# An expert's four table entries read in one load, one job ahead, by TensorE, ACT and DVE

## The chip, the core and the metric

The kernel runs on one core of one Trainium2 chip. The metric is the device time of one execution in microseconds (us). Engines are named as in the profile: PE is TensorE's matmul stream and PEld its weight loads, DVE is VectorE, ACT is ScalarE, POOL is GpSimd, SP is SyncE. A letter q behind a name (PEldq, DVEq) is that engine's sequencer, which reads instructions, works on registers and hands the rest to its engine.

## The reference, cut to what matters

The whole program is a two-layer block network on x (2 x 1024 tokens, 256 wide). The change touches one of its parts, the first mixture of experts: 16 experts, the best 4 of each token are used.

```python
def _L0_ffn_ref(x, keys, w1, b1, w2, b2, rw, rb):
    diff = x[:, :, None, :] - keys
    dist2 = jnp.sum(diff * diff, axis=-1)
    logits = -dist2 + jnp.einsum('bld,ed->ble', x, rw) + rb
    topv, topi = jax.lax.top_k(logits, TOP_K)
    w = jax.nn.softmax(topv, axis=-1)
    hidden = jax.nn.gelu(jnp.einsum('bld,efd->blef', x, w1) + b1, approximate=False)
    exp_out = jnp.einsum('blef,edf->bled', hidden, w2) + b2
    sel = jnp.take_along_axis(exp_out, topi[..., None], axis=2)
    return jnp.sum(w[..., None] * sel, axis=2)
```

F is 1024, so an expert is a 256 to 1024 to 256 network with a gelu between.

## The kernel before, in words

Two blocks matter, one behind the other, with a barrier of all engines between them.

**`route_phase`** (from line 1291) works out the gates and, on DVE and one partition, a small table `jobs` (int32, 1 x 220) from which the next block is steered. For each used expert in turn it has four entries: `n` (how many blocks of 256 tokens want it), `base` (how many jobs stand before it), `sel` (which expert it is) and `boff` (where its list of blocks stands), and it has the lists `blk` themselves and `pairs`, the number of pairs of experts. `JT` says where each kind begins: the four entries of one expert lie in four different arrays. Here too ACT splits the first expert's weights into a high part (L1340, L1343), and DVE makes the low part of w1 (L1463).

**`experts_phase`** runs jobs, one for each expert and block of 256 tokens. With these inputs there are 37 jobs for eight experts, which have 7, 2, 2, 8, 1, 8, 8 and 1 of them. Each of PE, ACT and DVE runs its own copy of the same nest, `jobs` (L1509): a hardware loop over pairs, in it the two experts of a pair written out (q = 0 and 1, with two sets of weights `ew_0` and `ew_1`), and in each a hardware loop over the expert's n jobs. At the head of each expert the engine reads the four entries with `entry` (`value_load`, L1475), at the head of each job one more, the block's number:

```python
n = entry(eng, "n", p * 2 + q, NB)
base = entry(eng, "base", p * 2 + q, E0 * NB)
sel = entry(eng, "sel", p * 2 + q, E0 - 1)
boff = entry(eng, "boff", p * 2 + q, E0 * NB - 1)
with eng.Fori(0, n) as j:
    blk = entry(eng, "blk", boff + j, NB - 1)
```

What an engine does in a job:

- PE (L1578): 48 matmuls up (8 hidden tiles x 2 halves of the width x 3 products of high and low parts), then 48 down in four groups of 12. Group g down waits for DVE's low part g (semaphore `e_lo`).
- ACT (L1608): eight Gelu activations of 128 x 256, two for a pair of hidden tiles (L1615), from PSUM to `hT`.
- DVE (L1628): for each of the four pairs a cast to the high part (L1633) and a subtraction for the low part (L1635), 128 x 512 each, both from SBUF to SBUF; at the end two updates of X (L1641) from PSUM.

POOL works beside them. At its start it adds eight pieces to X (L1567). Then `split` prepares the weights of the expert after next into the set that has come free: it waits for the last job of that set's expert (`e_down`), then runs a small operation on `eb` (L1541), four casts and four subtractions of 128 x 512 for w1 (L1545, L1551), a small one (L1555), four casts and four subtractions for w2 (L1557, L1561). SP loads the weights from HBM (L1480 to L1482), after POOL's eight adds at first. All matmuls of this block go through a helper, so their line is L1470.

Of the kernel before, what the change touches and what calls it, by code (L numbers as in the profile page):

```python
# [14 lines left out]
ALU = mybir.AluOpType  # L15
# [1235 lines left out]

JT = dict(sel=0, n=17, base=33, free=49, pairs=66, boff=67, blk=84)
JOB = 256
# [4 lines left out]
def route_phase(nc, k):  # L1258
# [4 lines left out]
    with ExitStack() as ctx:  # L1263
# [27 lines left out]
        @block.tensor  # L1291
        def _(pe):
            pe.wait_ge(k.r_G, 1)
            for j in range(EB):
                for w in range(NW):
                    last = nc.tensor.matmul(ps[32 * w:32 * w + 32, LG, :], G[:, j, :], k.hT[:, j, w * W:(w + 1) * W],
                                            start=(j == 0), stop=(j == EB - 1))
            last.then_inc(k.r_lgT, 1)
            pe.wait_ge(k.r_k2, 1)
            for j in range(EB):  # L1300
                last = nc.tensor.matmul(ps[:, KK, 0:E0], k.const("ones"), k2[:, j, :], start=(j == 0),
                                        stop=(j == EB - 1))
            last.then_inc(k.r_kk, 1)
            pe.wait_ge(k.r_lgE, 1)
            for t in range(4):
                last = nc.tensor.transpose(ps[:, LGT, t * P:(t + 1) * P], lgT[:, t * P:(t + 1) * P], k.const("ident"))
            last.then_inc(k.r_lg, 1)
            pe.wait_ge(k.r_wd, 1)
            nc.tensor.matmul(ps[:, CNT, 0:NT * E0], k.const("ones"), k.wE[:, :, :].rearrange("p e i -> p (e i)"),
                             start=True, stop=True).then_inc(k.r_cnt, 1)  # L1310
            for g in range(NW):
                for t in range(4):
                    last = nc.tensor.transpose(ps[0:E0, TR[g], t * P:(t + 1) * P], k.wE[:, :, 4 * g + t],
                                               k.const("ident"))
# [49 lines left out]
        def _(dve):  # L1364
# [27 lines left out]
            for i in range(NT):  # L1392
# [28 lines left out]

            sel, n = sn[:, 0, :], sn[:, 1, :]
            then(nc.vector.tensor_scalar(nj[:, 1, 0:E0 // 2], n[:, 0:E0:2], 0.0, None, ALU.is_gt))
            then(nc.vector.tensor_reduce(one[:, 0:1], nj[:, 1, 0:E0 // 2], AX.X, ALU.add))
# [10 lines left out]
            then(nc.vector.tensor_tensor(hot[:, 1, :], hot[:, 1, :], hot[:, 0, :], ALU.mult))  # L1435
            then(nc.vector.tensor_tensor(jf[:, JT["sel"]:JT["sel"] + E0], sel, hot[:, 1, :], ALU.add))
            then(nc.vector.tensor_scalar(hot[:, 2, :], hot[:, 0, :], one[:, 3:4], None, ALU.mult))
            then(nc.vector.scalar_tensor_tensor(jf[:, JT["boff"]:JT["boff"] + E0], jf[:, JT["sel"]:JT["sel"] + E0],
                                                float(NB), hot[:, 2, :], ALU.mult, ALU.add))
            then(nc.vector.tensor_tensor(n[:, 0:1], n[:, 0:1], one[:, 2:3], ALU.subtract))  # L1440
            jn, jb = jf[:, JT["n"]:JT["n"] + E0], jf[:, JT["base"]:JT["base"] + E0]
# [3 lines left out]
            nc.vector.memset(jf[:, JT["sel"] + E0:JT["n"]], 0.0)  # L1445
            nc.vector.memset(jf[:, JT["boff"] + E0:JT["blk"]], 0.0)
            nc.vector.memset(jf[:, JT["free"]:JT["free"] + 2], 0.0)
            nc.vector.tensor_tensor(jf[:, JT["free"] + 2:JT["free"] + E0 + 1], jf[:, JT["base"] + 1:JT["base"] + E0],
                                    jf[:, JT["base"] + 1:JT["base"] + E0], ALU.max)

# [3 lines left out]
            for e in range(E0):  # L1454
# [19 lines left out]
def job_entry(eng, k, name, at, limit):  # L1474
    return eng.value_load(k.jobs[0:1, bass.ds(at + JT[name], 1)], min_val=0, max_val=limit)  # L1475

# [8 lines left out]
def experts_phase(nc, k):  # L1485

    ps = k.ps
    with ExitStack() as ctx:
# [19 lines left out]

        def jobs(eng, each):  # L1509

            pairs = entry(eng, "pairs", 0, E0 // 2)
            with eng.Fori(0, pairs) as p:
                for q in range(2):
                    n = entry(eng, "n", p * 2 + q, NB)
                    base = entry(eng, "base", p * 2 + q, E0 * NB)
                    sel = entry(eng, "sel", p * 2 + q, E0 - 1)
                    boff = entry(eng, "boff", p * 2 + q, E0 * NB - 1)
                    with eng.Fori(0, n) as j:
                        blk = entry(eng, "blk", boff + j, NB - 1)
                        each(base + j, q, blk, p, sel)  # L1520

# [54 lines left out]
        def _(pe):  # L1576
            pe.sem_inc(k.e_down, TILES)

            def job(n, q, blk, p, sel):
                tok = bass.ds(blk * JOB, JOB)  # L1580
                pe.wait_ge(k.e_s1, p * 2 + (q + 1))
                for f in range(FB):
# [19 lines left out]

            jobs(pe, job)

        @block.scalar
        def _(act):
            act.sem_inc(k.e_act, FB)

            def job(n, q, blk, p, sel):
                for f in range(FB):  # L1610
# [6 lines left out]

            jobs(act, job)

        @block.vector  # L1620
        def _(dve):
# [5 lines left out]

            def job(n, q, blk, p, e):  # L1628
                dve.wait_ge(k.e_down, n * TILES + TILES)
                for g in range(PAIRS):  # L1630
# [3 lines left out]
                    dve.wait_ge(k.e_dhi, n * PAIRS + (g + 1))  # L1634
                    nc.vector.tensor_tensor(lo[:, f, :], hid[:, f, :], hi[:, f, :], ALU.subtract).then_inc(k.e_lo, 1)  # L1635
                dve.wait_ge(k.r_b2, NT // 2)
                for t in range(TILES):
# [7 lines left out]
                                    ALU.subtract).then_inc(k.e_s2, 1)  # L1645
            jobs(dve, job)

# [762 lines left out]
def network(nc, d):  # L2410
# [5 lines left out]
    with ExitStack() as ctx:  # L2416
# [42 lines left out]
        k.q_U, k.q_sum, k.q_D, k.q_out, k.q_pool, k.q_ex, k.q_exp = first("q_U q_sum q_D q_out q_pool q_ex q_exp")  # L2459
        k.q_dex, k.m_tz, k.s_mw2, k.p_w, k.p_wh = first("q_dex m_tz s_mw2 p_w p_wh")  # L2460
        k.q_den, = first("q_den")
        k.p_in, k.p_inh, k.p_hi, k.p_lo = first("p_in p_inh p_hi p_lo")
# [189 lines left out]
```

## Time and profile before

| | |
|---|---|
| runs | 1634.88, 1633.23, 1629.04 us; median 1633.23 |
| profiled execution | 1631.35 us, of which the span of the trace is 1629.2 |
| busy, share of the span | PE 85%, PEld 71%, DVE 61%, ACT 38%, POOL 31% |
| mean granted clock of TensorE | 0.92 of full speed |
| first mixture's jobs | from 580.26 us (first matmul) to 1034.33 us (start of the last) |

The profile comes from one execution. Idle time of an engine is put down to what released it; "issue" means that the profile shows nothing that the engine waited for, so that its own sequencer was late. A matmul's record is longer than its share of the stream: in an even stretch each lasts 0.28 us and the next starts 0.12 us after it.

### The profile page before, as it was taken

Reading aid. Unit: us, or ns where it says so; the run is one execution under the profiler, and the core shown is the slowest. Engines: PE = TensorE matmul, PEld = TensorE weight load, DVE = VectorE, ACT = ScalarE, POOL = GpSimd, SP = SyncE. Lnnn points to the kernel's source line nnn. Section 1 sums busy time; section 2 is a strip of 40 time slices with the busy share of each in tenths; the row PEclk is TensorE's granted clock in tenths of the full one; section 3 lists DMA queues with packets and bytes.
Section 4 is the critical chain, followed back from the end, with each engine's and each line's share of the span. In section 5 each row is a group of like instructions: output and inputs, shape, how many; then the busy total and the mean of one; then the engine's idle time right before and its main releaser. Section 6 shows DMA issues by size and latency. Waiting matters only on the chain. (4 is left out here: it accounts for less than half of the span.)

```text
span 1629.2 us, 24852 instructions
## 1 busy us (share of the span) xinstructions
PE 1385.6 (85%) x8658; PEld 1150.9 (71%) x8659; DVE 989.0 (61%) x1797; ACT 623.9 (38%) x1286; POOL 509.6 (31%) x483
## 2 busy tenths in 40 slices
PE   8849699877998679899989999798998996809992
PEld 3426366566975469889989999546887886509992
DVE  4864799757547655565455544676787784135653
ACT  3425867413222134223223333124565552215550
POOL 1330299442000370470070310722113100044673
PEclk9977799997998689999999999999999998859996
DMA  6000000001000121111020000000000000254423
GB/s 220 0 0 1 13 1 1 1 1 52 1 1 1 52 104 52 52 52 52 0 103 0 0 0 0 26 1 1 1 1 1 1 1 0 78 205 150 179 77 111
DMA packets 25243, 64.89 MB, mean 40 GB/s; under 512 B 4354, under 2 KB 16532, under 8 KB 20242
## 3 DMA queue, kind: packets, MB, share of 16 engines
q1 hardware_dynamic: 23634, 59.85, 10.3%
q0 software_dynamic: 1536, 4.10, 0.8%
q8 instruction: 42, 0.69, 0.2%
q14 instruction: 31, 0.25, 0.0%
HBM read 54.07 MB, written 9.44 MB: 39 GB/s over the span
## 5 line engine op out<-in xcount | busy, mean ns | idle before, releaser
L1615 ACT ACTIVATE hT<-ps,eb 128x256 f32<-128x256 f32 x296 | 124.4, 472 | 290.3 <-PE ps L1470 290.3
L1633 DVE CAST ehidh<-hT 128x512 fp32r<-128x512 f32 x148 | 79.5, 537 | 101.6 <-ACT hT L1615 101.6
L1936 ACT ACTIVATE pr<-ps,nmax 128x256 f32<-128x256 f32 (+7 forms) x128 | 94.1, 739 | 104.4 <-DVE nmax L1966 104.3
L1470 PE MATMUL ps<-kh,qz 128*128 128x512 f32 (+3 forms) x384 | 125.5, 381 | 3.4 <-ACT pr L1936 1.9
L1635 DVE TENSOR_TENSOR ehidl<-hT,ehidh 128x512 fp32r<-128x512 f32 x148 | 125.0, 844 | 5.1
L1641 DVE SCALAR_TENSOR_TENSOR X<-ps,wE,X 128x256 f32 x74 | 35.9, 485 | 113.6 <-PE ps L1470 104.1
L1541 POOL TENSOR_TENSOR eb<-eb1s,consts 128x8 f32<-128x8 f32 x8 | 1.6, 203 | 309.8 <-PE ps L1470 303.1
L1470 PE MATMUL ps<-hTh,ew_0h 128*128 x288 | 82.8, 288 | 18.4 <-issue 18.4
L1470 PE MATMUL ps<-hTh,ew_1h 128*128 x304 | 87.2, 287 | 9.7 <-issue 9.7
L1966 DVE TENSOR_REDUCE nmax<-ps 128x1 f32<-128x256 f32 (+7 forms) x128 | 91.2, 749 | 2.5 <-PE ps L1876 2.0
L1470 PE MATMUL ps<-ew_1h,ehidh 128*128 128x256 f32 x304 | 86.3, 284 | 3.4 <-DVE ehidl L1635 2.9
L1470 PE MATMUL ps<-hTh,ew_1l 128*128 x304 | 86.5, 285 | 0.0
L1470 PEld LDWEIGHTS ps<-kh,qz 128*128 128x128 f32 x384 | 76.7, 200 | 13.6 <-ACT pr L1936 4.9
L1470 PE MATMUL ps<-hTl,ew_1h 128*128 x304 | 86.0, 283 | 0.0
L1470 PE MATMUL ps<-ew_1l,ehidh 128*128 128x256 f32 x304 | 85.2, 280 | 0.0
L1470 PE MATMUL ps<-ew_1h,ehidl 128*128 128x256 f32 x304 | 85.2, 280 | 0.0
L1470 PE MATMUL ps<-ew_0h,ehidh 128*128 128x256 f32 x288 | 81.3, 282 | 3.6 <-DVE ehidl L1635 3.2
L1805 POOL CAST qz<-qh 32x256 fp32r<-32x256 f32 x64 | 27.9, 436 | 175.5 <-PE ps L1876 156.0
L1470 PE MATMUL ps<-hTh,ew_0l 128*128 x288 | 82.0, 285 | 0.0
L1470 PE MATMUL ps<-hTl,ew_0h 128*128 x288 | 81.8, 284 | 0.0
L1896 PE MATMUL ps<-v,hT 128*128 128x64 f32 x576 | 76.8, 279 | 5.6 <-ACT hT L1927 5.4
L1470 PE MATMUL ps<-ew_0l,ehidh 128*128 128x256 f32 x288 | 80.3, 279 | 0.0
(517 smaller groups left out, 4281.9 us busy)
## 6 DMA issues: line engine op xcount, KB each, us to landing
ew1s<-in_ew_dram SPq DMA_DIRECT2D x9, 1024.0 KB, 4.7
ew2s<-in_ew_dram SPq DMA_DIRECT2D x9, 1024.0 KB, 6.9
fw1s<-in_fw_dram SPq DMA_DIRECT2D x8, 1024.0 KB, 5.0
fw2s<-in_fw_dram SPq DMA_DIRECT2D x8, 1024.0 KB, 7.1
slot_rows<-zero SPq DMA_DIRECT2D x1, 2560.0 KB, 9.5
xr<-slot_rows SPq DMA_DIRECT2D x5, 512.0 KB, 5.9
xT<-in_xT_dram SPq DMA_DIRECT2D x4, 512.0 KB, 7.6
X<-in_x_dram SPq DMA_DIRECT2D x1, 2048.0 KB, 18.8
```

Of the source, the lines that this page charges most:

```text
L1470: last = nc.tensor.matmul(out, lhs[a], rhs[b], start=(start and n == 0), stop=(stop and n == 2), **kw)
L1541: nc.gpsimd.tensor_tensor(b1[q][:, :], b1s[q][:, :], k.const("ones", 0, FB), ALU.mult)
L1615: nc.scalar.activation(hid[:, f, :], ps[:, f // 2, (f % 2) * JOB:(f % 2 + 1) * JOB], ACT.Gelu, bias=b1[q][:, f:f + 1]).then_inc(k.e_act, 1)
L1633: nc.vector.tensor_copy(hi[:, f, :], hid[:, f, :]).then_inc(k.e_dhi, 1)
L1635: nc.vector.tensor_tensor(lo[:, f, :], hid[:, f, :], hi[:, f, :], ALU.subtract).then_inc(k.e_lo, 1)
L1641: nc.vector.scalar_tensor_tensor(x, ps[:, DOWN + t, 0:E], wE2[:, bass.ds(e * NT + blk * TILES + t, 1)], x, ALU.mult, ALU.add).then_inc(k.e ...
L1805: last = nc.gpsimd.tensor_copy(k.qz[r, i % QZ, n, :, s, :], part[r, :, i * P:(i + 1) * P])
L1896: last = nc.tensor.matmul(ps[:, PV + i % 2, h * 64:(h + 1) * 64], dT[:, n % 2, j, :], k.v[:, i - c + j, h * 64:(h + 1) * 64], start=(h == ...
L1936: nc.scalar.activation(pr[:, n % 3, u, 0:wide], half(n, u, wide), ACT.Exp, bias=nmax[:, n % 2, u:u + 1], accum_out=sums[:, u, n:n + 1]).th ...
L1966: nc.vector.tensor_reduce(nmax[:, n % 2, u:u + 1], half(n, u, wide), AX.X, ALU.max, negate=True).then_inc(k.a_max, 1)
```

## The change

The table keeps the four entries of an expert side by side (`ROW`, at 4 x the expert's number), so that one `reg_load` of four values brings them into four fixed registers. There are two such sets, for q = 0 and 1. Each engine reads expert 0's set ahead of the loops, and every job reads the set of the *following* expert into the other registers: PE between its up and its down part, ACT ahead of its activations, DVE after its four subtractions. At the head of an expert nothing is read; `snap` takes the registers' values over. PE reads its first set and `pairs` at the end of `route_phase` already, behind a new semaphore `r_jobs` that DVE raises with the table's last write; ACT and DVE read theirs at the start of `experts_phase`. SP and POOL keep their reads.

```diff
-JT = dict(sel=0, n=17, base=33, free=49, pairs=66, boff=67, blk=84)
+ROW = ("n", "base", "sel", "boff")
+JT = dict(free=4 * (E0 + 1), pairs=5 * (E0 + 1), blk=5 * (E0 + 1) + 1)
...
+            pe.wait_ge(k.r_jobs, 1)
+            k.pe_rows = [[pe.alloc_register(f"row_{q}_{name}") for name in ROW] for q in range(2)]
+            pe.reg_load(k.pe_rows[0], k.jobs[0:1, 0:4])
+            k.pe_pairs = job_entry(pe, k, "pairs", 0, E0 // 2)
...
-            nc.vector.tensor_copy(k.jobs[:, :], jf[:, :])
+            nc.vector.tensor_copy(k.jobs[:, :], jf[:, :]).then_inc(k.r_jobs, 1)
...
-        def jobs(eng, each):
-
-            pairs = entry(eng, "pairs", 0, E0 // 2)
+        def jobs(eng, rows, pairs, each):
+
+            def load_row(s, q):
+                eng.reg_load(rows[q], k.jobs[0:1, bass.ds(s * 4, 4)])
+
             with eng.Fori(0, pairs) as p:
                 for q in range(2):
-                    n = entry(eng, "n", p * 2 + q, NB)
-                    base = entry(eng, "base", p * 2 + q, E0 * NB)
-                    sel = entry(eng, "sel", p * 2 + q, E0 - 1)
-                    boff = entry(eng, "boff", p * 2 + q, E0 * NB - 1)
+                    n = eng.snap(rows[q][0], min_val=1, max_val=NB)
+                    base = eng.snap(rows[q][1], min_val=0, max_val=E0 * NB)
+                    sel = eng.snap(rows[q][2], min_val=0, max_val=E0 - 1)
+                    boff = eng.snap(rows[q][3], min_val=0, max_val=E0 * NB - 1)
                     with eng.Fori(0, n) as j:
                         blk = entry(eng, "blk", boff + j, NB - 1)
-                        each(base + j, q, blk, p, sel)
+                        each(base + j, q, blk, p, sel, lambda: load_row(p * 2 + (q + 1), 1 - q))
...
@@ PE, in a job, behind the 48 matmuls up
+                load_next()
                 pe.wait_ge(k.e_s2, p * 2 + (q + 3))
...
@@ ACT, in a job, ahead of the activations
+                load_next()
...
@@ DVE, in a job, behind the four subtractions
+                load_next()
                 dve.wait_ge(k.r_b2, NT // 2)
```

In `route_phase` the DVE operations that fill the table now write every fourth element, and two memsets of its padding became one.

How this moves PE's instructions. First the head of the second expert of a pair, before (ISA rows are register operations; the branch ends the first expert's loop, the twelve rows end in the loop's set-up, and the job's own read of `blk` comes behind them):

```order
L1518 COMPARE_AND_BRANCH
L1475 ISA
L1475 TENSOR_LOAD jobs
L1475 ISA x3
L1475 TENSOR_LOAD jobs
L1475 ISA x3
L1475 TENSOR_LOAD jobs
L1475 ISA x3
L1475 TENSOR_LOAD jobs
L1475 ISA x2
L1518 UNCONDITIONAL_BRANCH
L1518 ISA
```

The same place in the changed kernel, down to the job's first matmul:

```order
L1525 COMPARE_AND_BRANCH
L1521 ISA
L1525 UNCONDITIONAL_BRANCH
L1525 ISA
L1480 TENSOR_LOAD jobs
L1480 ISA x2
L1593 ISA
L1596 ISA
L1474 ISA
L1474 MATMUL ps<-hTh,ew_1h 128x256
```

Four loads with their eleven register rows have gone, one register row stands in their place, and the read of `blk` is the only load left on the way.

Second, PE between the last matmul up and the first one down in a job of q = 0, before:

```order
L1470 MATMUL ps<-hTl,ew_0h 128x256
L1470 MATMUL ps<-hTh,ew_0l 128x256
L1592 REGISTER_ALU
L1593 ISA
L1595 ISA
L1470 MATMUL ps<-ew_0h,ehidh 128x256
```

and in the changed kernel:

```order
L1474 MATMUL ps<-hTl,ew_0h 128x256
L1474 MATMUL ps<-hTh,ew_0l 128x256
L1517 ISA
L1517 TENSOR_LOAD jobs
L1605 REGISTER_ALU
L1606 ISA
L1608 ISA
L1474 MATMUL ps<-ew_0h,ehidh 128x256
```

One register row and one load of four values now stand ahead of the waits, in each of the 37 jobs.

## Rows read from the trace of the kernel before

**Rows 1.** The page's groups: busy, mean ns of one, idle before and its releaser
```profile
L1470 PE MATMUL ps<-hTh,ew_0h 128*128 x288 | 82.8, 288 | 18.4 <-issue 18.4
L1470 PE MATMUL ps<-hTh,ew_1h 128*128 x304 | 87.2, 287 | 9.7 <-issue 9.7
```

**Rows 2.** The block's start: PE's sequencer loads, then the timeline: start, duration, what
```profile
L1475 PEldq TENSOR_LOAD <-jobs x6: 301/309/484, 574.9 to 579.2; - x6
...
580.26 0.57 PE L1470 MATMUL ps<-hTh,ew_0h 128*128 x1 [10.66 <-issue]
...
581.53 4.80 POOL L1567 TENSOR_TENSOR X<-X,ew2s 128x512 f32<-128x512 f32 x4
...
583.22 0.84 ACT L1615 ACTIVATE hT<-ps,eb 128x256 f32<-128x256 f32 x2 [2.80 <-PE ps L1470]
```

**Rows 3.** Sequencers by line, 660 to 668 us: durations in ns, first and last start
```profile
L1518 PEldq ALU_OP  x1: 32/32/32, 660.3 to 660.3; - x1
L1475 PEldq TENSOR_LOAD <-jobs x4: 297/302/304, 660.7 to 662.9; - x4
L1475 DVEq TENSOR_LOAD <-jobs x5: 299/310/316, 663.2 to 666.2; - x5
```

**Rows 4.** Timeline of PE at the same change of experts
```profile
662.20 0.28 PE L1470 MATMUL ps<-ew_0h,ehidl 128*128 128x256 f32 x1
...
664.90 0.38 PE L1470 MATMUL ps<-hTh,ew_1h 128*128 x1 [2.43 <-issue]
```

**Rows 5.** PE's sequencer and stream inside an expert, 775 to 784 us
```profile
L1518 PEldq ALU_OP  x1: 32/32/32, 775.4 to 775.4; - x1
...
L1475 PEldq TENSOR_LOAD <-jobs x1: 299/299/299, 775.9 to 775.9; - x1
...
777.46 0.28 PE L1470 MATMUL ps<-hTh,ew_1h 128*128 x1
...
L1593 PEldq FUSED_REGOPS  x1: 42/42/42, 781.1 to 781.1; - x1
...
783.12 0.28 PE L1470 MATMUL ps<-ew_1h,ehidh 128*128 128x256 f32 x1
```

**Rows 6.** Timeline of POOL, PE and DVE behind the change at 924 us
```profile
924.08 0.20 POOL L1541 TENSOR_TENSOR eb<-eb1s,consts 128x8 f32<-128x8 f32 x1 [77.49 <-PE ps L1470]
...
926.58 0.38 PE L1470 MATMUL ps<-hTh,ew_0h 128*128 x1 [2.58 <-issue]
...
936.32 1.65 DVE L1635 TENSOR_TENSOR ehidl<-hT,ehidh 128x512 fp32r<-128x512 f32 x1
...
939.52 0.39 PE L1470 MATMUL ps<-hTh,ew_0h 128*128 x1
```

**Rows 7.** Timeline at the last change: POOL's start, the last matmul
```profile
1019.02 0.20 POOL L1541 TENSOR_TENSOR eb<-eb1s,consts 128x8 f32<-128x8 f32 x1 [77.41 <-PE ps L1470]
...
1034.33 0.28 PE L1470 MATMUL ps<-ew_1h,ehidl 128*128 128x256 f32 x1
```

**Rows 8.** Timeline of the first expert's second job, 593 to 607 us
```profile
593.03 0.21 POOL L1541 TENSOR_TENSOR eb<-eb1s,consts 128x8 f32<-128x8 f32 x1 [6.70 <-DMA eb1s<-in_eb_dram]
593.04 0.29 PE L1470 MATMUL ps<-hTh,ew_0h 128*128 x1
...
600.86 0.39 PE L1470 MATMUL ps<-ew_0h,ehidh 128*128 128x256 f32 x1 [0.64 <-DVE ehidl L1635]
...
606.78 0.38 PE L1470 MATMUL ps<-hTh,ew_0h 128*128 x1
```

**Rows 9.** A stretch: us, PE, PEld, DVE, ACT and POOL busy, clock, DMA share, GB/s
```profile
777.46:788.78 11.32, 11.32 (x99) 11.32 (x97) 5.46 (x11) 3.36 (x8) 0.00 (x0) 1.00 0.00 0
```

**Rows 10.** Timeline around the expert of one job and the one behind it
```profile
829.11 0.19 POOL L1541 TENSOR_TENSOR eb<-eb1s,consts 128x8 f32<-128x8 f32 x1
...
830.09 0.58 PE L1470 MATMUL ps<-hTh,ew_1h 128*128 x1 [2.85 <-issue]
...
844.55 0.38 PE L1470 MATMUL ps<-hTh,ew_1h 128*128 x1
```

More of the change, by code:

```diff
@@ L1422, in _ @@
             sel, n = sn[:, 0, :], sn[:, 1, :]
+            rows = {name: jf[:, at:4 * (E0 + 1):4] for at, name in enumerate(ROW)}
             then(nc.vector.tensor_scalar(nj[:, 1, 0:E0 // 2], n[:, 0:E0:2], 0.0, None, ALU.is_gt))
@@ L1435, in _ @@
             then(nc.vector.tensor_tensor(hot[:, 1, :], hot[:, 1, :], hot[:, 0, :], ALU.mult))
-            then(nc.vector.tensor_tensor(jf[:, JT["sel"]:JT["sel"] + E0], sel, hot[:, 1, :], ALU.add))
+            then(nc.vector.tensor_tensor(rows["sel"][:, 0:E0], sel, hot[:, 1, :], ALU.add))
             then(nc.vector.tensor_scalar(hot[:, 2, :], hot[:, 0, :], one[:, 3:4], None, ALU.mult))
-            then(nc.vector.scalar_tensor_tensor(jf[:, JT["boff"]:JT["boff"] + E0], jf[:, JT["sel"]:JT["sel"] + E0],
+            then(nc.vector.scalar_tensor_tensor(rows["boff"][:, 0:E0], rows["sel"][:, 0:E0],
                                                 float(NB), hot[:, 2, :], ALU.mult, ALU.add))
             then(nc.vector.tensor_tensor(n[:, 0:1], n[:, 0:1], one[:, 2:3], ALU.subtract))
-            jn, jb = jf[:, JT["n"]:JT["n"] + E0], jf[:, JT["base"]:JT["base"] + E0]
+            jn, jb = rows["n"][:, 0:E0], rows["base"][:, 0:E0]
             then(nc.vector.tensor_scalar(jn, n, 1.0, None, ALU.max))
@@ L1444, in _ @@
             then(nc.vector.tensor_tensor(jb, jb, jn, ALU.subtract))
-            nc.vector.memset(jf[:, JT["sel"] + E0:JT["n"]], 0.0)
-            nc.vector.memset(jf[:, JT["boff"] + E0:JT["blk"]], 0.0)
+            nc.vector.memset(jf[:, E0 * 4:E0 * 4 + 4], 0.0)
             nc.vector.memset(jf[:, JT["free"]:JT["free"] + 2], 0.0)
-            nc.vector.tensor_tensor(jf[:, JT["free"] + 2:JT["free"] + E0 + 1], jf[:, JT["base"] + 1:JT["base"] + E0],
-                                    jf[:, JT["base"] + 1:JT["base"] + E0], ALU.max)
+            nc.vector.tensor_tensor(jf[:, JT["free"] + 2:JT["free"] + E0 + 1], jb[:, 1:E0], jb[:, 1:E0], ALU.max)
             then(nc.vector.tensor_tensor(a[:, :, :], a[:, :, :], down[:, :].unsqueeze(1).to_broadcast([1, E0, NB]),
@@ L1474, in job_entry @@
 def job_entry(eng, k, name, at, limit):
-    return eng.value_load(k.jobs[0:1, bass.ds(at + JT[name], 1)], min_val=0, max_val=limit)
+    at = at * 4 + ROW.index(name) if name in ROW else at + JT[name]
+    return eng.value_load(k.jobs[0:1, bass.ds(at, 1)], min_val=0, max_val=limit)
 def load_first_mixture(sp, k, e, q):
@@ L1507, in following, with first_row @@
             return (p * 2 + 1, 1, p + 1) if q == 0 else (p * 2 + 2, 0, p + 2)
-        def jobs(eng, each):
-            pairs = entry(eng, "pairs", 0, E0 // 2)
+        def jobs(eng, rows, pairs, each):
+            def load_row(s, q):
+                eng.reg_load(rows[q], k.jobs[0:1, bass.ds(s * 4, 4)])
             with eng.Fori(0, pairs) as p:
                 for q in range(2):
-                    n = entry(eng, "n", p * 2 + q, NB)
-                    base = entry(eng, "base", p * 2 + q, E0 * NB)
-                    sel = entry(eng, "sel", p * 2 + q, E0 - 1)
-                    boff = entry(eng, "boff", p * 2 + q, E0 * NB - 1)
+                    n = eng.snap(rows[q][0], min_val=1, max_val=NB)
+                    base = eng.snap(rows[q][1], min_val=0, max_val=E0 * NB)
+                    sel = eng.snap(rows[q][2], min_val=0, max_val=E0 - 1)
+                    boff = eng.snap(rows[q][3], min_val=0, max_val=E0 * NB - 1)
                     with eng.Fori(0, n) as j:
                         blk = entry(eng, "blk", boff + j, NB - 1)
-                        each(base + j, q, blk, p, sel)
+                        each(base + j, q, blk, p, sel, lambda: load_row(p * 2 + (q + 1), 1 - q))
+        def first_row(eng, name):
+            rows = [[eng.alloc_register(f"{name}_{q}_{column}") for column in ROW] for q in range(2)]
+            eng.reg_load(rows[0], k.jobs[0:1, 0:4])
+            return rows
         @block.sync
@@ L1577, in _, with job @@
             pe.sem_inc(k.e_down, TILES)
-            def job(n, q, blk, p, sel):
+            def job(n, q, blk, p, sel, load_next):
                 tok = bass.ds(blk * JOB, JOB)
@@ L1601, in job @@
                             last.then_inc(k.e_down, 1)
-            jobs(pe, job)
+            jobs(pe, k.pe_rows, k.pe_pairs, job)
         @block.scalar
@@ L1607, in _, with job @@
             act.sem_inc(k.e_act, FB)
-            def job(n, q, blk, p, sel):
+            def job(n, q, blk, p, sel, load_next):
+                load_next()
                 for f in range(FB):
@@ L1616, in job @@
                                          bias=b1[q][:, f:f + 1]).then_inc(k.e_act, 1)
-            jobs(act, job)
+            jobs(act, first_row(act, "act_row"), entry(act, "pairs", 0, E0 // 2), job)
         @block.vector
@@ L1626, in _, with job @@
             hi, lo = hidp
-            def job(n, q, blk, p, e):
+            def job(n, q, blk, p, e, load_next):
                 dve.wait_ge(k.e_down, n * TILES + TILES)
@@ L1645, in _ @@
                                     ALU.subtract).then_inc(k.e_s2, 1)
-            jobs(dve, job)
+            jobs(dve, first_row(dve, "dve_row"), entry(dve, "pairs", 0, E0 // 2), job)
 def laplace_phase(nc, k):
@@ L2460, in network @@
         k.q_dex, k.m_tz, k.s_mw2, k.p_w, k.p_wh = first("q_dex m_tz s_mw2 p_w p_wh")
+        k.r_jobs, = first("r_jobs")
         k.q_den, = first("q_den")
```

## The prediction

> **What bounds the kernel now.** The page comes first: PE is the busiest engine, and among its groups the two that stand at the head of a job are preceded by 18.4 and 9.7 us of idle time for which nothing but its own sequencer is named [rows 1]. The rest of PE's idle time in this block is under 7 us, all of it behind DVE. So the question is where those 28.1 us lie. The timeline puts 10.66 us of them ahead of the block's very first matmul [rows 2]. The remaining 17.4 us are seven gaps, one at each change of experts, of 2.21 to 2.85 us; one of them is shown from both sides [rows 4]. Counted from start to start and less one even step of 0.12 us it costs 664.90 - 662.20 - 0.12 = 2.58 us, 0.15 more than the idle time; all seven cost 17.4 + 7 x 0.16 = 18.6 us.
>
> The sequencer's rows say what fills a gap. PE's sequencer turns the loop at 660.3 us, 1.9 us ahead of the last matmul's start, and then reads the entries one by one: four loads from 660.7 to 662.9, a step of 2.2 / 3 = 0.75 us, although the load itself lasts 0.30 [rows 3]. The queued matmuls run out in the meantime. Inside an expert the same turn is made at 775.4 us for a matmul at 777.46, with one load (`blk`) on the way, and the stream has no break [rows 5].
>
> Then the view that decides how much of a gap is worth having. Behind each change POOL starts to split the next weights, at the old expert's last matmul. While it does, DVE's operations are stretched: a subtraction takes 1.65 us [rows 6], where in a job without POOL eleven operations of DVE together take 5.46, 0.5 each [rows 9]. The first job of an expert is therefore set by DVE: its last subtraction starts at 936.32, and the job takes 939.52 - 926.58 = 12.94 us [rows 6] where an undisturbed one takes 11.32 [rows 9].
>
> **The change, part by part.**
>
> *PE at a change of experts.* Four steps of 0.75 us go, 3.0 in all; a register row comes (some 0.1). The way from the loop's turn to the first matmul was 664.90 - 660.3 = 4.6 us and becomes 1.7. The old expert's stream lasts 662.20 + 0.12 - 660.3 = 2.0 us from there, so the gap closes. From the second expert of a pair to the next pair the outer loop's branch comes in too; those gaps were some 0.3 us longer, and 0.3 us of cover is left. So: seven gaps closed, 18.6 us on PE. DVE reads its entries behind its last update of X, five loads from 663.2 to 666.2 us [rows 3]; with one left it is ready near 664.3, and its first cast, 2.6 us behind the first matmul, can start at 662.3 + 2.6 = 664.9. ACT is idle at that time.
>
> *What is late next.* The first job of an expert starts 2.4 to 3.0 us earlier, while POOL starts where it did, 0.24 us behind PE's new start. DVE's eight operations now meet POOL from POOL's start on. The trace has one job just like that: the first expert's second job begins at 593.04, POOL at 593.03, and it lasts to 606.78, 13.75 us from POOL's start, with PE waiting for DVE on the way [rows 8]. At the change at 924 us the same count is 939.52 - 924.08 = 15.44 us [rows 6], at the last one 1034.33 + 0.11 - 1019.02 = 15.42 [rows 7]. A closed gap is thus worth 15.43 - 13.75 = **1.7 us**, not 2.6; some 1.0 us goes back to waits on DVE. Five changes (at 665, 692, 719, 927 and 1021 us) give 5 x 1.7 = 8.4.
>
> *The expert of one job* (814 to 830 us). Its own change gives 1.7. At the next one POOL is late by itself: it ends the one split and starts the other at 829.11, before PE's 830.09, and the job takes 14.46 us [rows 10]. In the changed kernel PE reaches this job some 4.5 us earlier, ahead of POOL's second split. No row shows that case. At most the gap (3.0) and all of the job's excess (14.46 - 11.32 = 3.1) go, 6.1 us; at least nothing goes, if everything behind hangs on POOL. Walking DVE's operations through POOL's by the durations above I get a job of some 13 us and a next job some 1.3 us longer than now, because POOL's second split reaches into it: 3.0 + 1.4 - 1.3 = 3.1. I take **2.5**, nearer the other changes. Together 4.2.
>
> *The start.* Of PE's six loads from 574.9 to 579.2 us [rows 2] five are read elsewhere: `pairs` with its step of 0.86 us, four entries with 3.1, less a register row, so PE starts **3.9 us** earlier, near 576.4. ACT drops from six reads to three and its look-ahead; its steps are 0.61 us, so it is ready near 579, and its first activation, 2.96 us behind the first matmul [rows 2], would come at 579.3: just covered. DVE is ready before that. But POOL's adds to X last until 586.3 [rows 2], and DVE's first pair would meet them from 580.2 instead of 584.1: four stretched operations in place of two. Bounds: 3.9 if DVE's delay stays covered, 0 if it hangs on POOL, whose split for the next expert starts a little later too. I take **1.8**.
>
> *Added work.* In each of 37 jobs PE has a register row and a load of four values. PE's sequencer reaches that place at 781.1 us, 2.0 ahead of the matmul it feeds at 783.12 [rows 5]. A load of one value lasts 0.30 us; four values cost between that and 4 x 0.30 = 1.2; both fit into 2.0. On ACT the load stands where it idles for 4 us or more, on DVE where it waits 1.4 us or more for PE. All at nothing; without the cover on PE it would be 37 x 0.75 = 28 us. The new wait on `r_jobs` stands behind all of PE's work in its block: the table is written at 562.6 us, PE's last matmul there ends at 569.6, and the barrier opens at 574.6, so nothing is queued behind it. DVE's every-fourth-element writes of 16 values lie in a stretch in which it then idles 9.5 us. SP and POOL keep their loads.
>
> The Trainium skill ("Runtime: NRT & Kernel Launch", Instruction fetch mechanics) puts a register load at about 200 ns per register even in bulk. By that the new load would cost 0.8 us, inside the bounds, and the sum would not move.
>
> **The sum.** 8.4 + 4.2 + 1.8 = 14.4 us. The profiled execution took 1631.35 us, so it becomes 1617.0; the median shown is 1.9 us above it, so I give 1633.2 - 14.4 = **1618.8 us**.
>
> **Rivals.**
>
> 1. *Everything is kept* (22.5 us = 18.6 + 3.9: 1610.7 us). For it: DVE's contended time depends on which of POOL's operations it meets, and PE would spend less time at half clock behind gaps. Against it: rows 8 show PE waiting 0.64 us and more for DVE in just this constellation.
>
> 2. *The first jobs hang on POOL altogether.* Two changes with gaps that differ by 0.37 us ended 15.44 and 15.42 us after POOL's start [rows 6, 7]: the earlier start was worth nothing there. If that went on, only scraps at the start and at 830 us would be left, some 3 us: 1630. Against it stands the 13.75 of rows 8.
>
> 3. *The gap is not the loads.* If PE were held by fetching its code at the loop's ends, the gap would stay: 1633. Against it: the sequencer's rows follow one another through the whole gap [rows 3], and only 0.3 us differs between falling through and branching back. The Trainium skill (same page and section) says that a taken branch outside the fetched window stalls until the code arrives. By that page the gaps behind a jump back would stay; by the rows they don't come from it.
>
> 4. *Slower: the look-ahead load breaks PE's stream in every job.* If the sequencer let the queue run dry around a load of four values, each job would pay a step, 0.75 us: 37 x 0.75 = 28 us, less 14.4, gives 1647. It decides from 14.4 / 37 = 0.39 us a job. For it: no load of four values is in the trace, nor any load at this place. Against it: the load of `blk` stands in the same stream 37 times, and no break of over 0.1 us is seen behind it inside an expert [rows 5].
>
> **How the numbers follow.** A measurement of this kernel can tell about 0.5% from no change, 8.2 us. The forecast has 0.71; its own range is 7 to 19 us of gain, and 0.05 of its chance lies under 8.2. Rival 1 has 0.11, rival 2 0.09, rival 3 0.04, rival 4 0.05. Faster by over 0.5%: 0.66 + 0.11 = 0.77. Within: 0.05 + 0.09 + 0.04 = 0.18. Slower: 0.05. The range reaches from rival 1 (1610) to a gain of 6 us (1627), and leaves out rivals 2 to 4.
>
> **What would show it.** Right: "issue" ahead of the first matmuls of a job falls from 28.1 us to about 7 (the start alone); no idle time over 0.2 us at the seven changes; first jobs of an expert that last 13.7 to 14.2 us, with PE's waits for DVE's low part grown from 6 us to over 12; a first matmul that now comes 5.7 us behind the barrier coming 1.8 behind it. Wrong: gaps of 0.3 us or more in the middle of jobs (rival 4); gaps that stay at every change, or at those behind a jump back (rival 3); first jobs of 15.4 us (rival 2) or under 13 (rival 1).

## The result, and the profile after

The changed kernel takes 1618.49 us, the median of 4 runs (1615.93 to 1620.65), against 1632.16 us of the kernel before (4 runs, 1629.04 to 1634.88). The ratio is 0.991, with a 95% interval of 0.989 to 0.993: 13.7 us, faster by 0.7% to 1.1%. The profiled execution took 1619.42 us, its span 1617.3.

The page's groups of the changed kernel that answer to [rows 1], with the two of DVE that feed the second half of a job (busy, mean ns of one, idle before and its releaser):

```profile
L1649 DVE TENSOR_TENSOR ehidl<-hT,ehidh 128x512 fp32r<-128x512 f32 x148 | 132.7, 897 | 5.1
L1647 DVE CAST ehidh<-hT 128x512 fp32r<-128x512 f32 x148 | 90.0, 608 | 73.4 <-ACT hT L1629 73.3
...
L1474 PE MATMUL ps<-ew_1h,ehidh 128*128 128x256 f32 x304 | 86.2, 284 | 8.5 <-DVE ehidl L1649 8.2
L1474 PE MATMUL ps<-ew_0h,ehidh 128*128 128x256 f32 x288 | 82.1, 285 | 8.3 <-DVE ehidl L1649 8.0
L1474 PE MATMUL ps<-hTh,ew_0h 128*128 x288 | 82.3, 286 | 7.0 <-issue 7.0
...
L1474 PE MATMUL ps<-hTh,ew_1h 128*128 x304 | 85.5, 281 | 0.1
```

The 28.1 us of "issue" ahead of a job's first matmul are 7.0, and those 7.0 are the block's start. In their place PE waits 8.2 + 8.0 = 16.2 us for DVE's low part, where it waited 6.1 before. DVE's two operations have the same work as before and are longer: 897 ns for a subtraction (844 before), 608 for a cast (537 before).

The timeline of the changed kernel at the change that [rows 4] show from before, with DVE's first four operations and PE's two waits:

```profile
662.69 0.28 PE L1474 MATMUL ps<-ew_0h,ehidl 128*128 128x256 f32 x1
662.81 0.28 PE L1474 MATMUL ps<-hTh,ew_1h 128*128 x1
...
663.06 0.20 POOL L1553 TENSOR_TENSOR eb<-eb1s,consts 128x8 f32<-128x8 f32 x1 [49.49 <-PE ps L1474]
...
665.30 0.48 DVE L1647 CAST ehidh<-hT 128x512 fp32r<-128x512 f32 x1 [1.44 <-ACT hT L1629]
...
665.82 1.67 DVE L1649 TENSOR_TENSOR ehidl<-hT,ehidh 128x512 fp32r<-128x512 f32 x1
...
667.41 1.54 DVE L1647 CAST ehidh<-hT 128x512 fp32r<-128x512 f32 x1
...
668.98 1.67 DVE L1649 TENSOR_TENSOR ehidl<-hT,ehidh 128x512 fp32r<-128x512 f32 x1
...
670.71 0.39 PE L1474 MATMUL ps<-ew_1h,ehidh 128*128 128x256 f32 x1 [0.66 <-DVE ehidl L1649]
...
673.29 0.39 PE L1474 MATMUL ps<-ew_1h,ehidh 128*128 128x256 f32 x1 [0.95 <-DVE ehidl L1649]
```

The new expert's first matmul follows the old one's last after 0.12 us, the even step. POOL starts 0.25 us behind it, DVE's operations take 1.5 to 1.7 us beside it, and PE waits in the second half of the job. The job ends at 676.58: 13.76 us.

The start and the end of the block in the same timeline. The first row answers to [rows 2], the others to [rows 7]; the last row of each kernel is the first matmul behind the block.

```profile
577.49 0.57 PE L1474 MATMUL ps<-hTh,ew_0h 128*128 x1 [6.96 <-issue]
...
1019.39 4.95 POOL L1573 TENSOR_TENSOR ew_0l<-ew2s,ew_0h 128x512 fp32r<-128x512 f32 x4
...
1020.26 0.28 PE L1474 MATMUL ps<-ew_1h,ehidl 128*128 128x256 f32 x1
1026.11 1.30 PE L443 MATMUL ps<-consts,X 128*128 128x128 f32 x5 [5.57 <-PEq L2539]
```

The same place in the kernel before:

```profile
1031.02 5.49 POOL L1561 TENSOR_TENSOR ew_0l<-ew2s,ew_0h 128x512 fp32r<-128x512 f32 x4
...
1038.27 3.93 PE L443 MATMUL ps<-consts,X 128*128 128x128 f32 x21 [3.66 <-PEq L2523]
```

In both kernels the next block's first matmul comes 1.77 us behind the end of POOL's last split (1019.39 + 4.95 = 1024.34 to 1026.11, and 1036.51 to 1038.27), not behind PE's last matmul. The idle time of PE there grew by 1.9 us.

From here on a stretch of PE from the last matmul ahead of the experts' block to the first one behind it is called the block. It took 1038.27 - 568.98 = 469.3 us before and 1026.11 - 569.90 = 456.2 us after, 13.1 less. Outside it the two profiled executions took 1159.9 and 1161.1 us, and those of the variants below 1158 to 1163 us (once 1166), so the gain lies in the block.

### The profile page after: what moved, and what is told of

Same layout as the page of the kernel before. It is cut to its first block and busy times, and to the rows that moved or that the text cites. A ratio compares the mean times of both kernels' runs of the same rounds, so it can differ in the third digit from the quotient of the medians.

```text
span 1617.3 us, 24732 instructions
## 1 busy us (share of the span) xinstructions
PE 1382.0 (85%) x8658; PEld 1147.4 (71%) x8659; DVE 1006.8 (62%) x1796; ACT 623.7 (39%) x1286; POOL 511.7 (32%) x483
## 5 line engine op out<-in xcount | busy, mean ns | idle before, releaser
L1649 DVE TENSOR_TENSOR ehidl<-hT,ehidh 128x512 fp32r<-128x512 f32 x148 | 132.7, 897 | 5.1
L1647 DVE CAST ehidh<-hT 128x512 fp32r<-128x512 f32 x148 | 90.0, 608 | 73.4 <-ACT hT L1629 73.3
L1474 PEld LDWEIGHTS ps<-kh,qz 128*128 128x128 f32 x384 | 77.5, 202 | 13.7 <-ACT pr L1951 4.7
```

What stands on the lines that cost most here:

```text
L1474: last = nc.tensor.matmul(out, lhs[a], rhs[b], start=(start and n == 0), stop=(stop and n == 2), **kw)
L1647: nc.vector.tensor_copy(hi[:, f, :], hid[:, f, :]).then_inc(k.e_dhi, 1)
```

## The experiments

All variants of the changed kernel have one register operation more than it, which cuts the base off at zero. The first run adds this operation alone, and the others are measured against it.

**The yardstick.**

```
-                    base = eng.snap(rows[q][1], min_val=0, max_val=E0 * NB)
+                    base = eng.snap(smax(eng.snap(rows[q][1]), 0), min_val=0, max_val=E0 * NB)
```

> The changed kernel with one more register operation on each engine at an expert's head: the base is cut off below at zero. It is the yardstick for the other variants of the changed kernel. Every theory expects the changed kernel's time, 1618.5 us, and at most 0.2 us at each of seven changes of expert above it: 1618 to 1620 us.

Measured: 1617.5 us, ratio to before 0.991 (0.989 to 0.993). The block took 456.5 us, 0.3 more than that of the changed kernel.

**TensorE alone, and the others alone.** The two kernels halve the change. In the first, ACT and DVE have the old `jobs`, with four `entry` reads at the expert's head; in the second TensorE has it, and its two reads in `route_phase` are gone.

```
-            jobs(act, first_row(act, "act_row"), entry(act, "pairs", 0, E0 // 2), job)
+            jobs_old(act, job)
...
-            jobs(dve, first_row(dve, "dve_row"), entry(dve, "pairs", 0, E0 // 2), job)
+            jobs_old(dve, job)
```

```
-            jobs(pe, k.pe_rows, k.pe_pairs, job)
+            jobs_old(pe, job)
```

> TensorE as in the changed kernel (four entries in one load, ahead of the change); ACT and DVE read the four entries one by one at the expert's head, as before. Theory A (at a change DVE's chain of casts sets the end of the first job, and POOL's split takes back part of what an earlier start gives): DVE would be ready 3.52 us behind its last X update, as in the kernel before, where in the changed kernel its first cast came 1.44 us behind it. So the first cast comes 2.1 us later; by what before and after showed (first cast 3.2 us earlier, job's end 1.85 us earlier) a first job ends 0.9 to 1.2 us later, six times: 5.4 to 7.3 us above the yardstick, near 1625 us. Theory B (only TensorE's own reads were in the way, DVE's lie beside its wait for ACT): the yardstick's time, 1618 to 1620 us.

> ACT and DVE as in the changed kernel; TensorE reads the four entries one by one at the expert's head, and its pairs and first row in the experts' block, as before. Theory A and B: TensorE stands idle some 2.5 us at each change again, the first cast waits for it, and nothing is gained: 1631 to 1633 us, the kernel before. A theory by which the engines' reads each bear a part would put it at about 1625 us; one by which the gain is the placement of the program and not the reads cannot say, but would not have it fall on the kernel before.

Measured: TensorE alone 1629.7 us (0.998, 0.997 to 1.000), the others alone 1632.24 us (1.000, 0.998 to 1.001). The second is as expected. The first is not: it is 12 us above the yardstick, where 5.4 to 7.3 were expected, and most of the gain is gone. The timeline of this kernel, with TensorE alone changed, behind the same change of experts, here at 661.4 us:

```profile
661.39 0.29 PE L1474 MATMUL ps<-hTh,ew_1h 128*128 x1
...
661.99 0.49 DVE L1669 SCALAR_TENSOR_TENSOR X<-ps,wE,X 128x256 f32 x1 [0.26 <-DVE X L1669]
...
666.11 0.86 DVE L1660 CAST ehidh<-hT 128x512 fp32r<-128x512 f32 x1 [3.63 <-ACT hT L1642]
...
668.69 0.39 PE L1474 MATMUL ps<-ew_1h,ehidh 128*128 128x256 f32 x1 [1.52 <-DVE ehidl L1662]
```

ACT's activations were there at 663.84; what DVE did for 3.63 us was read the table. Its first cast comes 4.7 us behind PE's first matmul, where in the changed kernel it comes 2.5 behind, and PE has used up its first half of the job and waits 1.5 us before the second half can begin at all. The cast comes 2.2 us later, as the expectation had it, but the first job of this expert takes 15.70 us and so ends 1.9 us later, not 0.9 to 1.2. All seven first jobs behind a change take 15.4 to 15.9 us, as much as idle time and job took together in the kernel before (2.6 + 13.0 at this change). What TensorE alone kept is 2.6 us of the block: 0.9 up to the start of the fourth job and 1.8 at the expert of one job, from the old expert's last matmul to the end of the third job behind it (42.84 us, 44.68 before). At the other changes neither half of the change brings anything by itself.

**The row read at the expert's head.** One load of four, but no look-ahead.

```
                 for q in range(2):
+                    load_row(p * 2 + q, q)
...
-                        each(base + j, q, blk, p, sel, lambda: load_row(p * 2 + (q + 1), 1 - q))
+                        each(base + j, q, blk, p, sel, lambda: None)
```

> The four entries in one load on all three engines, but read at the expert's head and not in the job in front. One load step on TensorE's sequencer takes 0.45 to 0.75 us (0.31 us the load, the rest around it), and at a change of the changed kernel its sequencer is ready just when the last matmul starts (lead 0). Theory A: each of the seven changes shows an idle time of about 0.5 us, six of them count: 3 us above the yardstick (2 to 4.5 us), near 1622 us. Theory C (the gap needs the look-ahead, since any load at the head waits for the engine's queue to empty): the gap of about 2 us comes back, and the time is near 1630 us.

Measured: 1619.02 us (0.992, 0.990 to 0.994), 1.5 us above the yardstick; the block is 459.1 us, 2.6 above. From the last matmul of an expert to the first of the next it is 0.23 to 0.94 us from start to start at the seven changes, 0.64 at the one near 689 us. These are the idle times of theory A, but they cost less than its 3 us: the first jobs behind them are shorter (13.43 and 13.46 us near 689 and 916, where the yardstick's take 13.88 and 13.90). Of the 2.6 us in the block some 1.3 are the pace of undisturbed jobs (last section). So most of the gain is four reads made one, and the look-ahead adds about 1.3 us, half of it at the block's start.

**POOL kept quiet.** In both kernels alike POOL's casts and subtractions, and its additions to X at the block's start, were cut to a column each, and TensorE always used the first expert's weights:

```
-                        last = nc.gpsimd.tensor_copy(w1[q][0][:, j, at], w1s[q][:, j, at])
+                        last = nc.gpsimd.tensor_copy(w1[1][0][:, j, c * W:c * W + 1], w1s[q][:, j, c * W:c * W + 1])
...
-                                        [w[:, j, f * P:(f + 1) * P] for w in w1[q]],
+                                        [w[:, j, f * P:(f + 1) * P] for w in w1[0]],
```

> The kernel before with POOL's work in the experts' block cut to one column per instruction (instructions and semaphores are kept): it leaves out the splitting of every expert's weights but the first expert's, which TensorE uses for all, and all but one column of the addition of the second biases. The phases behind it run on other data, so it is compared with its partner and by its own experts' block. Both theories: no job longer than 11.3 us, 37 jobs in 418.5 us, seven idle times of about 2.45 us and 5.7 us at the start; the block some 16 us shorter than the 460 us before.

> The same cut of POOL's work in the changed kernel (with the base cut off at zero); it leaves out what its partner leaves out. Theory A (POOL's split takes back part of each idle time removed): with POOL quiet the whole of it shows: 7 x 2.45 + 3.7 = 20.9 us less than its partner (18.5 to 22). Rival (what was not gained was never there: the other part of the idle time moved elsewhere on TensorE or the first jobs are long for a reason other than POOL): the difference stays 13 to 15 us, and first jobs longer than 11.5 us remain.

Measured: 1618.88 us and 1589.58 us, 29.3 apart where 20.9 were expected. The blocks are 457.1 and 431.2 us long, 25.9 apart; the spans of the two profiled executions differ by 28.3, and the 2.4 us outside the block are within the differences named above. In the changed kernel's version every job behind the first lasts 11.31 to 11.41 us, so it is POOL's work that makes first jobs long in the changed kernel. The kernel before misses its expectation: its block is 12.2 us shorter than with POOL at work, not 16, and four of its first jobs behind a change last 12.7 to 12.9 us, not 11.3. It has a second loss that the expectation left out. The view by stretches shows it (us, then PE, PEld, DVE, ACT and POOL busy, granted clock, DMA share, GB/s). Kernel before with POOL quiet: the first half of a first job, twice behind an idle time.

```profile
664.47:671.73 7.26, 7.26 (x48) 7.26 (x49) 2.58 (x5) 2.51 (x6) 0.43 (x3) 0.76 0.70 259
...
717.75:723.50 5.75, 5.75 (x48) 5.75 (x49) 2.58 (x5) 2.52 (x6) 0.61 (x4) 1.00 0.58 196
```

The kernel before itself, in the same halves of first jobs, and the second halves behind two of them:

```profile
664.90:672.16 7.26, 7.26 (x49) 7.26 (x49) 4.06 (x5) 2.52 (x6) 7.18 (x8) 0.76 0.01 2
672.16:677.96 5.80, 5.78 (x51) 5.53 (x49) 4.35 (x6) 0.84 (x2) 5.72 (x6) 1.00 0.00 0
...
718.82:724.57 5.75, 5.75 (x49) 5.75 (x49) 3.13 (x3) 2.52 (x6) 5.67 (x5) 1.00 0.00 0
724.57:732.12 7.55, 6.39 (x51) 5.72 (x49) 6.06 (x7) 0.84 (x2) 7.47 (x9) 1.00 0.00 0
```

And the changed kernel:

```profile
662.81:668.47 5.66, 5.66 (x50) 5.66 (x49) 3.92 (x5) 2.52 (x6) 5.33 (x7) 1.00 0.01 3
668.47:676.58 8.11, 6.39 (x51) 5.74 (x49) 6.62 (x7) 0.84 (x2) 8.03 (x9) 1.00 0.00 0
```

With POOL quiet, the granted clock fell from 2.4 to 1.2 GHz behind four of the seven idle times of some 2.5 us, for so long that the half took 7.26 us instead of 5.66: 1.6 us, 6.4 in all. With 18.1 us of gaps and 3.8 at the start, less 1.6 for seven jobs that ran at a shorter step and 0.4 in the first job, that makes 26.3, against the 25.9 measured.

In the kernel before proper the same fall is there at 665, 692 and 830 us. At 665 us PE takes 1.6 us longer in the first half and then waits hardly at all for DVE (5.80 us); at 719 the clock stays, and the second half is 1.9 us longer than an undisturbed one, with waits for DVE (7.55). Either way the job takes 12.9 to 13.3 us (the one at 830 us, with POOL late, 14.46). PE's slow stretch and DVE's lag covered one another. That is so only while the slow stretch is short. In the kernel before without its last split (next experiment) the clock was low for longer behind the change at 923 us, and that first job took 15.33 us, where it takes 12.94 in the kernel before [rows 6]:

```profile
922.66:931.16 8.50, 8.50 (x49) 8.50 (x50) 4.60 (x5) 2.53 (x6) 8.47 (x9) 0.64 0.00 0
931.16:937.99 6.83, 5.73 (x50) 5.50 (x49) 5.37 (x5) 2.12 (x3) 6.35 (x5) 1.00 0.00 0
```

In the changed kernel there is neither such an idle time nor a fall at the changes of experts, and the whole of DVE's lag shows: 8.11 us for the second half.

**The last split left out.** SP and POOL no longer load and split the weights of a ninth expert.

```
-            with sp.Fori(0, pairs) as p:
+            sp.wait_ge(k.e_s2, 2)
+            load_first_mixture(sp, k, entry(sp, "sel", 1, E0 - 1), 1)
+            with sp.Fori(1, pairs) as p:
...
-            with pool.Fori(0, pairs) as p:
+            split(1, 1, 1)
+            with pool.Fori(1, pairs) as p:
                 for q in range(2):
-                    split(*following(p, q))
+                    split(*((p * 2, 0, p + 1) if q == 0 else (p * 2 + 1, 1, p + 1)))
```

> The kernel before without the last trip of the splitting: the weights of a ninth expert, which no job uses, are neither loaded nor split; the split of the second expert stands ahead of the loop. Theory A (the block's closing barrier waits for that split, and its work slows the last job): the last job falls from 13.3 us to 11.3 us, the idle time behind the last matmul from 3.66 us to about 2: 3.6 us less than before, near 1628.5 us. Rival (the split ends in time, the idle time behind the last matmul is the barrier's own): 2 us less at most, 1630 to 1632 us.

> The same in the changed kernel (with the base cut off at zero). Theory A: the last job falls from 13.7 us to 11.3 us, and the idle time behind the last matmul from 5.57 us to about 2: 5.9 us less than the changed kernel, near 1613 us, and 15.5 to 16.5 us below its partner, where the pair without this edit stood 13.7 us apart: the last change of expert is now worth its share. Rival: both of the pair gain the same, the distance stays 13.7 us, and the time is near 1616 us.

Measured: the kernel before so edited 1628.16 us (0.998, 0.996 to 0.999), 3.4 below the 1631.56 of the runs beside it, expected 3.6; the changed kernel so edited 1610.71 us (0.987, 0.985 to 0.989), 6.8 below the yardstick, expected 5.9. They are 17.4 us apart, with 13.7 between the unedited ones in the first comparison, where 15.5 to 16.5 were expected. The medians are good to some 3 us, so the trace has to carry the point. The end of the block in the changed kernel without the last split:

```profile
1018.68 0.28 PE L1474 MATMUL ps<-ew_1h,ehidl 128*128 128x256 f32 x1
1021.58 0.76 PE L443 MATMUL ps<-consts,X 128*128 128x128 f32 x3 [2.62 <-PEq L2541]
```

and in the kernel before without it:

```profile
1035.35 0.88 PE L443 MATMUL ps<-consts,X 128*128 128x128 f32 x3 [2.63 <-PEq L2525]
```

The idle time behind the last matmul is now the same in both, 2.6 us, where it was 3.66 and 5.57. The changed kernel's last job, 13.73 us long with POOL splitting, takes 11.31, the time of an undisturbed job:

```profile
1007.49:1018.80 11.31, 11.31 (x98) 11.27 (x96) 5.44 (x11) 3.36 (x8) 0.00 (x0) 1.00 0.00 0
```

In the kernel before the last job does not fall to the 11.3 us expected but takes 12.91, since the clock fell behind the idle time there (0.76 in the job's first half). So its 3.4 us agree with the 3.6 by luck: from the seventh expert's last matmul to the next block it gains 19.60 - 18.19 = 1.4 us, and some 1.3 us more of its block are six jobs at the shorter pace (last section). In the changed kernel the same stretch falls from 19.58 us to 14.21, 5.4 us. With the last split the two kernels end the block alike (19.60 and 19.58); without it they are 4.0 us apart, 2.4 of the gap and 1.6 of the clock. So the last split did set the block's end in both kernels, and it took from the changed kernel what the last change of experts had gained. The rival is out: 1.0 and 2.9 us of the idle time behind the last matmul were the split's. The edit also gives a kernel that is faster than both, by 21 us against the kernel before.

**More loads in a job.** The look-ahead load on TensorE was repeated:

```
-                load_next()
+                for _ in range(7):
+                    load_next()
```

> The changed kernel (base cut off at zero) with the look-ahead load on TensorE issued three times in each job in place of once. The load took 0.33 us there and a step of one about 0.45 us, and the sequencer was still 1.4 us ahead of the first matmul behind it. Theory A (the sequencer's lead hides it): 0.9 us more fits into 1.4 us, so nothing changes: 1618 to 1620 us. Rival (each such load delays the stream by itself): 37 jobs by 0.9 us, 33 us more, near 1652 us.

> The same with the look-ahead load issued seven times in each job. Theory A: six more steps of 0.45 us are 2.7 us, 1.3 us more than the lead; an idle time of about 1.3 us ahead of the first down matmul in every job, 37 of them, 48 us less what first jobs absorb: 1650 to 1670 us. Should the lead be really deeper than read (over 2.7 us): 1618 to 1620 us. If each load delayed the stream by itself: 37 x 2.7 = 100 us more, near 1719 us.

Measured: 1622.42 us and 1620.06 us, with blocks of 455.4 and 455.8 us. These two say nothing on the question. The sequencer's rows of the kernel with seven loads show one in a job:

```profile
L1517 PEldq TENSOR_LOAD <-jobs x1: 332/332/332, 752.4 to 752.4; - x1
```

Loads into the same registers from the same place had been folded into one in building. (The first is 4.9 us above the yardstick, but its block is 1.1 us shorter; in its trace the difference lies behind the block.) So the loads were given something to do:

```
                 load_next()
+                for i in range(6):
+                    pe.reg_load(k.pe_zero, k.jobs[0:1, E0 * 4 + i:E0 * 4 + i + 1])
+                    pe.reg_add(k.pe_rows[1 - q][1], k.pe_rows[1 - q][1], k.pe_zero)
```

> In the two runs with repeated look-ahead loads the trace showed one load of L1517 in a job, not three or seven: repeats into the same registers had been folded into one. Here TensorE reads, behind the look-ahead load, two other entries of the table that hold zero, and adds each to the next base, so that none can be dropped. In the yardstick the sequencer began this place at 753.81 us and had the queue's next weight load at 755.80, with 1.25 us left behind its last row. Theory A: two steps of some 0.5 us fit, nothing changes, 1617 to 1620 us. Rival (the lead is smaller than read, or each load stops the stream): 37 x 1.0 us, 1654 us.

> Six such reads behind the look-ahead load. Theory A: 6 x 0.5 = 3.0 us, 1.75 more than the 1.25 us left: an idle time of about 1.75 us ahead of the first down matmul in the 28 or so jobs that do not wait for DVE there anyway, 50 us, and up to 1.6 us more in each if the granted clock falls behind it, as it fell behind four of the seven idle times of 2.5 us and more in the kernel before with POOL quiet: 1665 to 1710 us. Rival (the sequencer can run much further ahead than 2 us): 1617 to 1620 us.

Measured: 1618.1 us with two (0.991, 0.988 to 0.994), and 1655.43 us with six (1.013, 1.011 to 1.016). The sequencer's rows of a job of the second, which begins at 750.60:

```profile
L1607 PEldq TENSOR_LOAD <-jobs x6: 299/302/314, 754.6 to 757.0; - x6
```

and PE's timeline there:

```profile
757.62 0.38 PE L1475 MATMUL ps<-ew_1h,ehidh 128*128 128x256 f32 x1 [1.25 <-DVE ehidl L1653]
```

The step from one load to the next is (757.0 - 754.6) / 5 = 0.48 us. Two more cost nothing, six more break the stream by 1.25 us in front of the second half of each job (the releaser named, DVE, had long been done: it is the sequencer). A job inside an expert is then 12.57 us, 1.3 to 1.5 more, and the kernel is 37 us slower. Theory A named the mechanism; its 1665 to 1710 us were too much by 10 at least. The idle time was taken 0.5 us too long, and the clock did not fall behind it: it is 1.00 in every job behind the first.

```profile
750.60:763.18 12.58, 11.33 (x98) 11.13 (x97) 5.45 (x11) 3.36 (x8) 0.00 (x0) 1.00 0.00 0
```

So the place has room for the look-ahead load and two more steps; rival 4 of the prediction sets in somewhere between two and six more.

## Why the prediction was right

The mechanism was right, but that the time, 1618.8 us, was met within 0.3 us is luck. The three terms 8.4, 4.2 and 1.8 measure 7.4, 3.7 and 1.3 us, 12.4 in place of 14.4. The measured gain is 13.7, with a pace of jobs in it that was not forecast, and the forecast started from a median of 1633.2 us, 1.0 above that of the four runs. One reason given was half wrong. Step by step:

- *The gaps are PE's four reads and close.* Right. All seven are gone (0.34 us at most from start to start), and a kernel that keeps only these reads loses the whole gain. The sequencer's way had to shrink from 4.6 to 1.7 us; it has almost nothing to spare at a change, as the 0.2 to 0.9 us with one more load there show.
- *What is late next is DVE beside POOL; first jobs of 13.75 us.* Right, and well sized: 13.76, 13.82, 13.77 and 13.76 us at four changes. With POOL quiet they are 11.3 to 11.4.
- *A closed gap is worth 15.43 - 13.75 = 1.7 us.* At the change at 913 us (927 before) it is 1.85: from the old expert's last matmul to the end of the job 13.95 us, before 15.80. The other three give 1.9 each. But "the first job of an expert is therefore set by DVE", said of the kernel before, is not true of all of them. Behind the changes at 665 and 692 us PE's stretch at half clock made the 13 us, and DVE's lag lay hidden under it. The difference of two whole stretches, which the forecast used, holds whichever it is.
- *DVE's reads* had no price in the sum, only the remark that DVE would be ready in time. They are worth as much as PE's: without their part of the change each first job but those around the expert of one job ends where it did before. (That run took ACT's part away as well; that DVE's is the one that counts is read from its trace, where ACT's output was ready 2.3 us ahead of the cast.) The forecast had the right state but would have misled anyone who meant to change TensorE alone.
- *Five changes.* This is the step that failed. The one at 1021 us gave nothing, since the block ends when POOL has split the weights of a ninth expert, and POOL started that with the last expert as before: PE's gap behind its last matmul grew from 3.66 to 5.57 us. The last job itself took the 13.7 us forecast. [Rows 7] show POOL's start and PE's last matmul, but not what the next block waited for. Four changes at 1.85 are 7.4 us against the 8.4 forecast for five. With the two terms below that makes 12.4 of the block's 13.1 us; the rest is of the size by which the pace of undisturbed jobs differs (last section).
- *The expert of one job, 2.5 + 1.7 = 4.2 us.* It gave 3.7: from the old expert's last matmul to the end of the third job behind it 44.68 us before (811.28 to 855.96) and 40.96 after (806.04 to 847.00). Its own change gave 1.96, the next one, for which 2.5 was taken, 1.76. The three jobs lasted 13.94, 14.17 and 12.73 us: the second is over the 13 forecast, the third bears the 1.3 us expected of POOL's second split.
- *The start, 1.8 us.* The first matmul came 2.00 us behind the barrier, 1.8 forecast, 5.70 before. To the start of the fourth job 1.34 us were left of the 3.7; DVE's lag beside POOL took most of the rest.
- *Added work at nothing.* Right. The load of four values lasts 0.33 us against 0.30 for one. The Trainium skill ("Runtime: NRT & Kernel Launch", Instruction fetch mechanics), by which a load has its price for each register also in bulk, would have made it 0.8 us, an estimate; the row says otherwise for this load from SBUF.

Rival 1 (everything is kept, 22.5 us) is what a quiet POOL gives, and even that is less than the 25.9 us of the block then, because of the clock. Rival 2 (first jobs hang on POOL) holds at one place alone, the last. Rival 3 (fetching code) is out: no gap stayed, neither behind a jump back nor elsewhere. Rival 4 needed more than 1 us (two steps of 0.48) on the sequencer beyond what the change adds.

## What to carry to other kernels

When a gap on one engine closes, look at what the engine that feeds it does in the same moment: here TensorE's and VectorE's table reads stood side by side, and taking away only one of them brought nothing at five of the seven changes. Read a row of registers in one load and a job early, in the engine's own slack. And ask of the last turn of a loop what its block's end really waits for: work prepared for a next item that never comes can hold the barrier, and it eats whatever the other engines gain in front of it.

## What was not expected of the hardware

- A register load of four values, in a job, takes 0.33 us on TensorE's sequencer, 0.31 on ACT's and 0.34 on DVE's (medians of 37). One of one value takes 0.31, 0.29 and 0.32 in the same kernel, so three more values cost 0.02 us.
- The granted clock fell to 1.2 GHz behind some idle times of 2.5 us and not behind others: with POOL quiet at 664, 691, 811 and 919 us but not at 717, 826 and 1014, with TensorE having run its usual even stream before each of them. In the kernel before it fell behind three of the seven, with ACT and DVE alone changed behind six, in the kernel before without the last split behind three others, near 812, 923 and 1020 us, each time in the one execution traced. Behind the 1.25 us of idle time in every job of the last experiment it did not fall. What decides between them stays open.
- An undisturbed job lasts 11.31 us in some stretches and 11.09 in others, in the same kernel and at a granted clock of 1.00 in both; which experts have the shorter jobs differs from trace to trace. The changed kernel:

```profile
847.00:858.09 11.09, 11.09 (x99) 11.09 (x97) 5.45 (x11) 3.35 (x8) 0.00 (x0) 1.00 0.24 98
938.77:950.09 11.32, 11.32 (x99) 11.32 (x98) 5.46 (x11) 4.64 (x9) 0.00 (x0) 1.00 0.00 0
```

The yardstick has seven such jobs and the kernel with two added loads eighteen, and its block is 2.6 us shorter. So this moves the time by 2 us and more, as much as a term of the sum, and single executions of two variants can't be compared closer than that. Nothing that was run tells its cause.
